# Attention scores of a transformer block: q and k kept fp32 on chip in 32-partition quadrants, in place of a three-way bf16 split stacked through DRAM

## What is computed

```python
q = split_heads(x @ Wq.T)            # (B, 16 heads, T, 16)
k = split_heads(x @ Wk.T)
v = split_heads(x @ Wv.T)
q = _apply_rope(q)                   # t * cos + rot(t) * sin
k = _apply_rope(k)
scores = jnp.einsum('bhtd,bhsd->bhts', q, k) * scale
scores = jnp.where(causal[None, None], -jnp.inf, scores)
attn = jax.nn.softmax(scores, axis=-1)
out = jnp.einsum('bhts,bhsd->bhtd', attn, v)
return out.transpose(0, 2, 1, 3).reshape(B, T, 256) @ Wo.T
```

## Time and profile before

| what | value |
|---|---|
| runs of the kernel | 3821.51 us median of 3 (3818.33 to 3827.86) |
| span of the profiled execution, first to last instruction | 3828.2 us |
| PE matmul busy | 3068.0 us, 80% |
| DVE busy | 2449.9 us, 64% |
| POOL busy | 1463.4 us, 38% |
| ACT busy | 1276.0 us, 33% |
| mean granted TensorE clock | 0.897 of 2.4 GHz |
| moved by DMA | 106.01 MB |

### The profile page before, as it was taken

One profiled execution on the slowest core, in us unless ns is written; L12 is line 12 of the kernel. 1 busy time (PEld: TensorE's weight loads), 2 busy tenths in 40 slices (PEclk: granted clock), 3 DMA queues, 4 the chain that ended last, 5 costly groups with the idle time before them and its releaser, 6 DMA issues. The chain is left out here.

```text
span 3828.2 us, 47386 instructions
## 1 busy us (share of the span) xinstructions
PE 3068.0 (80%) x17056; PEld 1877.3 (49%) x17056; DVE 2449.9 (64%) x5133; ACT 1276.0 (33%) x2632; POOL 1463.4 (38%) x1323
## 2 busy tenths in 40 slices
PE   2689767897688975899758997589885898858898
PEld 1235743456434564345633456335573355723557
DVE  5755767547585485854758547585575855768556
ACT  1353033530345312452125521255211542216422
POOL 2224442244513445134551345413454134541344
PEclk9799987999889987899978999789997999969999
DMA  4400023000330003200041000410005000050000
GB/s 129 78 2 1 1 59 64 2 1 1 67 56 2 1 1 78 45 2 1 1 93 30 1 1 1 96 28 2 0 1 109 15 2 0 7 115 2 1 1 12
DMA packets 46763, 106.01 MB, mean 28 GB/s; under 512 B 9713, under 2 KB 30225, under 8 KB 43281
## 3 DMA queue, kind: packets, MB, share of 16 engines
q1 hardware_dynamic: 46480, 102.24, 13.0%
HBM read 65.51 MB, written 35.91 MB: 26 GB/s over the span
## 5 line engine op out<-in xcount | busy, mean ns | idle before, releaser
L803 DVE TENSOR_REDUCE mxp<-PB 128x1 f32<-128x512 f32 (+3 forms) x1536 | 753.2, 549 | 274.7 <-PE PB L1053 182.2
L656 ACT ACTIVATE arena<-PB 128x512 f32<-128x512 f32 (+3 forms) x1536 | 650.5, 509 | 651.3 <-PE PB L1064 646.5
L1050 PE MATMUL PB<-arena 96*128 96x512 bf16 (+3 forms) x1536 | 542.7, 383 | 286.2 <-DMA arena<-parts 214.8
L535 POOL TENSOR_SCALAR_AFFINE_SELECT arena<-arena 128x512 f32<-128x512 f32 x256 | 162.7, 636 | 981.4 <-ACT arena L656 981.0
L1064 PE MATMUL PB<-arena 99*128 99x512 bf16 (+3 forms) x1536 | 467.6, 344 | 16.7 <-DMA arena<-augT 9.5
L1050 PEld LDWEIGHTS PB<-arena 96*128 96x128 bf16 x1536 | 160.8, 106 | 631.6 <-DVE mxp L803 349.2
L1079 PE MATMUL PB<-arena 128*32 128x512 f32 (+3 forms) x3072 | 343.4, 520 | 15.5 <-ACT attn L642 13.7
L1273 PE MATMUL PB<-arena 128*128 128x128 f32 x1792 | 243.4, 293 | 98.3 <-DVE arena L965 98.2
L520 POOL TENSOR_TENSOR hl<-arena,hh 128x512 fp32r<-128x512 f32 x192 | 248.6, 1295 | 192.5 <-ACT hh L673 192.5
L1135 PE MATMUL PB<-xh,wgu 128*128 128x512 f32 x768 | 306.9, 400 | 11.4 <-DVE xres L761 10.8
L1135 PE MATMUL PB<-xl,wgu 128*128 128x512 f32 x768 | 303.3, 395 | 0.0
(11 more groups left out here) (138 smaller groups left out, 5536.3 us busy)
## 6 DMA issues: line engine op xcount, KB each, us to landing
arena<-parts SPq DMA_DIRECT2D x112, 256.0 KB, 10.5
parts<-arena SPq DMA_DIRECT2D x96, 256.0 KB
arena<-parts SPq DMA_DIRECT2D x16, 768.0 KB, 16.0
xres<-in_x SPq DMA_DIRECT2D x16, 512.0 KB, 4.3
arena<-parts SPq DMA_DIRECT2D x16, 512.0 KB, 18.5
out<-xres SPq DMA_DIRECT2D x16, 512.0 KB, 2.9
wlow_dram<-wlow SPq DMA_DIRECT2D x1, 2304.0 KB, 6.8
arena<-augT SPq DMA_DIRECT2D x96, 8.0 KB, 1.8
```

Source lines behind the costliest of these rows:

```text
L656: act.activation(pt[:, U % 3, h, 0:n], bank("score", t)[:, 0:n], ACT.Exp, scale=DH ** -0.5).then_inc(act_emptied, 1)
L803: dve.reduce_max(mxp[:, g % 2, h, col:col + 1], bank("max", g * NPC + k)[:, 0:n], axis=AX.X).then_inc(dve_emptied, 1)
L1050: last = mm(ps[:, 0:n], qst[0:AUG, h, 128 * i:128 * i + 128], kst[0:AUG, h, s0:s0 + n], start=True, stop=not diag)
```

## The change

q and k are made in another layout: one product tile holds, for each of four heads, 16 partitions of q and then 16 of k, a quadrant of 32 partitions per head (the host interleaves the weights as `wqk`). DVE shuffles the tile by 8 channels (L719 of the changed kernel) and multiplies by cos into `qk` (L720); POOL multiplies by sin and adds (L466, L469). A second shuffle on DVE swaps the halves of each quadrant into `kq` (L727), which has k where `qk` has q. All of it is fp32. The bf16 split, the DRAM tensor, `qst`, `kst`, the memset of ones and ACT's part in this are gone; a DMA writes the row of ones in `kq`.

`max_items` (L981) and `score_items` (L1000) issue four heads after each other. Each is an fp32 product over 16 partitions (17 with the maximum's row) of another quadrant, so that the four heads lie in four row groups of the array. The four causal products follow the four heads. The negated maxima are one fp32 row: two small operations on DVE, a transpose in fp32 and four DMAs of 4 KB per group. In the plan of banks four max items stand together, then four score items.

```diff
+QK_ORDER = [(0, 0), (1, 0), (0, 1), (1, 1), (2, 0), (2, 1), (3, 0), (3, 1)]
+KEYS_READY = [3, 4, 6, 8]
+SWAP = [(i + 16) % 32 for i in range(32)]
-LAG = 12
-DELAY = NPC + LAG
+NQ = len(PIECES)
+LAG = 3
+DELAY = NQ + LAG
...
-    for t in range(NSC + DELAY):
-        if t < NSC:
-            p.append(("max", t, "dve"))
-        if NPC <= t < NSC + NPC and t % NPC == AUG_AT:
-            p.append(("aug", t // NPC - 1, "dve"))
+    for t in range(NG * NQ + DELAY):
+        if t < NG * NQ:
+            p.extend(("max", HG * t + h, "dve") for h in range(HG))
+        if NQ <= t < NG * NQ + NQ and t % NQ == 0:
+            p.append(("aug", t // NQ - 1, "dve"))
         if t >= DELAY:
-            p.append(("score", t - DELAY, "act"))
+            p.extend(("score", HG * (t - DELAY) + h, "act") for h in range(HG))
...
-        qst = take(8192, bf16, 0).rearrange("p (h t) -> p h t", h=NH)
-        kst = take(8192, bf16).rearrange("p (h t) -> p h t", h=NH)
+        qk = take(4096, f32, 0).rearrange("p (g t) -> p g t", g=NG)
+        kq = take(4096).rearrange("p (g t) -> p g t", g=NG)
...
+                    sp.wait_ge(keys_set, len(QK_ORDER))
+                    for h in range(HG):
+                        sp.dma_start(kq[32 * h + DH:32 * h + DH + 1, :, :],
+                                     consts[2].rearrange("a (g t) -> a g t", g=NG)).then_inc(ones_loaded, 16)
                     for g in range(NG):
                         wait_emptied(sp, "aug", g)
-                        for r in range(3):
-                            sp.dma_start(qst[AUG + r:AUG + r + 1, HG * g:HG * g + HG, :],
-                                         augT[32 * r:32 * r + 32, g % 2, :]).then_inc(aug_loaded[g], 16)
+                        for h in range(HG):
+                            sp.dma_start(qk[32 * h + DH:32 * h + DH + 1, g, :],
+                                         augT[NT * h:NT * h + NT, g % 2, :]).then_inc(aug_loaded[g], 16)
...
+                    for e, (g, f) in enumerate(QK_ORDER):
                         cols = slice(HALF * f, HALF * f + HALF)
+                        pool.wait_ge(rot_shuffled, e + 1)
+                        pool.tensor_tensor(turned[e % 2], turned[e % 2], rope[:, 1, cols], ALU.mult).then_inc(rot_sin, 1)
+                        pool.wait_ge(rot_sin, e + 1)
+                        wait_emptied(pool, "qk", e)
+                        pool.tensor_tensor(qk[:, g, cols], qk[:, g, cols], turned[e % 2], ALU.add).then_inc(roped, 1)
...
+                        dve.stream_shuffle(turned[e % 2], bank("qk", e)[:, :], ROTATE).then_inc(rot_shuffled, 1)
+                        dve.tensor_tensor(qk[:, g, cols], bank("qk", e)[:, :], rope[:, 0, cols],
+                                          ALU.mult).then_inc(dve_emptied, 1)
+
+                    def keys(e):
+                        g, f = QK_ORDER[e]
+                        cols = slice(HALF * f, HALF * f + HALF)
+                        dve.wait_ge(roped, e + 1)
+                        dve.stream_shuffle(kq[:, g, cols], qk[:, g, cols], SWAP).then_inc(keys_set, 1)
...
+                    def max_items(g, j):
+
+                        i, s0, n, col = PIECES[j]
+                        for h in range(HG):
+                            k = g * NPC + HG * j + h
+                            r = slice(32 * h, 32 * h + DH)
+                            diag = s0 + n == 128 * (i + 1)
+                            wait_bank(pe, "max", k)
+                            last = mm(bank("max", k)[:, 0:n], qk[r, g, 128 * i:128 * i + 128], kq[r, g, s0:s0 + n],
+                                      start=True, stop=not diag)
+                            if not diag:
+                                last.then_inc(filled, 1)
                         if diag:
+                            for h in range(HG):
+                                k = g * NPC + HG * j + h
+                                mm(bank("max", k)[:, n - 128:n], identb[:, :], causal[:, :],
+                                   start=False, stop=True).then_inc(filled, 1)
+
+                    def score_items(g, u):
+
                         j, f = UNITS[u]
                         t0 = max(HALF * f, 128 * j)
                         n = HALF * (f + 1) - t0
+                        for h in range(HG):
+                            k = g * NPC + HG * u + h
+                            r = slice(32 * h, 32 * h + DH + 1)
+                            wait_bank(pe, "score", k)
+                            mm(bank("score", k)[:, 0:n], kq[r, g, 128 * j:128 * j + 128], qk[r, g, t0:t0 + n],
+                               start=True, stop=True).then_inc(filled, 1)
```

More of the change, by code:

```diff
@@ L630, in _ @@
                     act.wait_ge(arena_set, 2)
-                    for e in range(4):
-                        high(e)
-                    mid(3)
                     for n in range(4):
                         v_out(n)
-                    for e in range(4, 8):
-                        high(e)
-                    mid(7)
                     def pv_out(g):
@@ L798, in _ @@
+                    def keys(e):
+                        g, f = QK_ORDER[e]
+                        cols = slice(HALF * f, HALF * f + HALF)
+                        dve.wait_ge(roped, e + 1)
+                        dve.stream_shuffle(kq[:, g, cols], qk[:, g, cols], SWAP).then_inc(keys_set, 1)
+                    for e in range(len(QK_ORDER)):
                         rotary(e)
+                        if e >= 2:
+                            keys(e - 2)
+                    keys(len(QK_ORDER) - 2)
@@ L1041, in v_item @@
                         last.then_inc(filled, 1)
-                    def max_item(g, k):
-                        h, (i, s0, n, col) = max_item_of(k)
-                        h += g * HG
-                        wait_bank(pe, "max", g * NPC + k)
-                        ps = bank("max", g * NPC + k)
-                        diag = s0 + n == 128 * (i + 1)
-                        last = mm(ps[:, 0:n], qst[0:AUG, h, 128 * i:128 * i + 128], kst[0:AUG, h, s0:s0 + n],
-                                  start=True, stop=not diag)
-                        if diag:
-                            last = mm(ps[:, n - 128:n], identb[:, :], causal[:, :], start=False, stop=True)
-                        last.then_inc(filled, 1)
-                    def score_item(g, k):
-                        u, h = k // HG, g * HG + k % HG
+                    def max_items(g, j):
[9 more added lines that the diff above has]
+                                last.then_inc(filled, 1)
+                        if diag:
+                            for h in range(HG):
[3 more added lines that the diff above has]
+                    def score_items(g, u):
                         j, f = UNITS[u]
@@ L1061, in score_item @@
                         n = HALF * (f + 1) - t0
-                        wait_bank(pe, "score", g * NPC + k)
-                        ps = bank("score", g * NPC + k)
-                        mm(ps[:, 0:n], kst[0:AUG + 3, h, 128 * j:128 * j + 128], qst[0:AUG + 3, h, t0:t0 + n],
-                           start=True, stop=True).then_inc(filled, 1)
+                        for h in range(HG):
+                            k = g * NPC + HG * u + h
[3 more added lines that the diff above has]
+                               start=True, stop=True).then_inc(filled, 1)
                     def pv(g, u):
@@ L1373 @@
         masks.append((p // (2 * m) == t // (2 * m)) & (p % (2 * m) < m))
+    arrays["one"] = np.ones((1, NG * T), np.float32)
     arrays["ci"] = np.concatenate(masks + [p == q], 1).astype(np.int32)
```

192 lines of the change are left out of this document (51 added, 141 removed).

## The result

| what | before | changed |
|---|---|---|
| time | 3824.69 us median of 4 runs (3818.33 to 3829.77) | 4643.74 us median of 4 runs (4641.87 to 4651.55) |
| ratio to before | | 1.2144, 95% interval 1.2126 to 1.2162 |
| span of the profiled execution | 3828.2 us | 4642.8 us |
| mean granted TensorE clock | 0.897 | 0.74 |

The change makes the kernel 21% slower. The forecast was 3950 us with a range from 3790 to 4250: the sign was right, the size was wrong by 694 us, and the time lies above the range.

A forecast was written before the change was run, and what follows sets the result against it. PE, or a chain through it, was taken to bound most stages. Per batch -20 (front) + 28 (mixed) + 5 (maxima) + 3 (scores) = +16 us, times eight +128, on 3821.5: 3950 us, range 3790 to 4250.

The forecast's parts named there:

- The front: From the q and k products to the first reduction: without split and DRAM trip, 20 us less per batch.
- The mixed stage: Where maxima, scores and `pv` mix: waits for banks make a step 3.65 us against 2.81, 28 us more per batch.
- rival 3: TensorE stays at 1.2 GHz in the mixed stage: +2.0 us a step, +65 per batch, 4470 us; chance 0.07.
- Maxima alone: Stage of row maxima only, before the first score: fills and reductions chain, +5 us per batch, bounds 0 and +12.
- Scores alone: Last stage of a batch: scores wait two by two for ACT, +3 us, bounds 0 and +5.
- Rival 1: Weight loads or passes of row groups queue on PE: 4130 us for loads, 4290 for passes; chance 0.15.
- rival 2: The row groups do not run side by side at all: mixed step 6.7 us, about 5000 us; chance 0.05.
- Rival 4: The bank wait does not bind, so a mixed step is PE's 2.57 us: 3600 us; chance 0.13.
- The tipping point: Length of a mixed-stage step under which the batch gains: 3.17 us.
- the forecast's sum of +16 us per batch: All attention stages of a batch: -20 + 28 + 5 + 3 = +16 us, times eight +128 us.

The follow-up runs named there:

- The bursts: The changed kernel with unused fp32 products of 512 columns ahead of the batch loop, in groups of 16 or 32 rows or all 128 rows, waiting for nothing: 4889.41 us.

## Why the prediction was wrong

- **The front, -20 us per batch** (bounds 18 to 21): -20.9. POOL's pair of operations, forecast 2.6 us, took 2.58, and the first reduction comes 37.8 us after the first statistics where "about 40" was said.
- **The mixed stage, 3.65 us a step** (3.25 to 4.1): 5.79, and this is the step that failed. Its chain was right: at the higher level it takes 3.77 us with the same waits, the last two score heads wait for the reductions of heads 0 and 1 as forecast, and halving these takes 0.42 us off. What failed is that each of its terms for PE came from rows at 2.4 GHz, on the premise that the stage would keep that clock. The stage ran at 1.2 GHz from end to end. That was **rival 3**, priced at 4470 us with a chance of 0.07. For this stage its price was near: it added +65 us per batch, and the clock's share measured here is +66.7. It left the last stage and the maxima out, and its reason, that TensorE would wait more, is only part of the cause.
- **Why rival 3 got 0.07.** The prediction judged the clock by waits: a stage with waits for ACT is granted 0.94, so this one would be too. Every product in those rows works on 96, 99 or 128 rows of the array. The change puts all row-group products on 16 or 17 rows of each 32, and no row of the trace before has such a one. The bursts show that this alone can keep the clock from rising, without any wait, and the kernel with 32 rows shows that undoing it alone brings the clock of the mixed stage back. Waits count beside it: the bursts of 16 rows behind full products hold 2.4 GHz, and the stage does not.
- **Maxima alone, +5 us** (0 to +12): +11.9, at the upper bound, which was set with the lower clock in mind. The causal products with their changes of shape carry it: without them it is 29.2 us even at 0.50. The rows do not: with 32 it is still +11.4.
- **Scores alone, +3 us** (0 to +5): +11.6, outside its bounds; with 32 rows +2.1. Again the clock.
- **Rival 1** (loads or passes queue) and **rival 2** (groups not side by side): refuted by eight loads in 0.52 us at the lower clock and 0.31 at the higher, and by 0.87 us for a round of four. **Rival 4** (the bank wait doesn't bind): refuted; at the full clock and with the banks in another order a step is 3.45 us still. The tipping point, 3.17 us, was passed by the kernel with bf16 maxima and full products alone, in its one batch at full clock: 102.5 / 33 = 3.11 us.
- With the clock out of the way in the mixed and the last stage, the forecast's sum of +16 us per batch stands against +24.6 in the kernel with 32 rows (-20.6 + 11.4 + 31.7 + 2.1), and 3950 us against 4031.

Where did the expected gain go? The 20.9 us of the front came back in full. At the higher clock the chain of the mixed stage takes 31.7 us away (21.3 with the other order of banks and no causal products), and the causal products cost 11.9 in the maxima-only stage; the lower clock then adds 66.7 us in the mixed stage and about 9.5 in the last.

**What stays open.** By what rule rows and waits together set the clock; the changes of shape were not varied apart from them. Whether the rows' contents matter (in the kernel with 32 rows the 15 rows added to the scores hold zeros in `kq` and k in `qk`, and yet the clock rose; rows of zeros on both sides weren't tried). What makes the clock drop for a few microseconds in the kernels with bf16 maxima was not found; the kernel before has such drops too (at 662.2 and 696.4 in the second batch). A seventh circulating bank wasn't tried, since `pv` holds the other two.

## What to carry to other kernels

When a change makes the products of a long stage narrower in rows of the array, price the stage at both clock levels, and look in the trace for products as narrow before trusting the clock of today. If a tile has unused rows, let the product run over them with zeros or constants on one side: a round of 512 columns took 0.87 us with 16 rows in each group and with 32, and here the extra rows were worth 613 us. And when groups of four share a ring of six banks, write down which item lies six places back for each: the two that fall on banks just filled put the reader's latency into every step.

## What the runs showed of the hardware

- Four row groups of 16 rows, fp32, without a gap for 34.5 us, did not lift TensorE from 1.2 to 2.4 GHz; four groups of 32 rows behind them were at 2.4 GHz after 4.6 us; one group of 32 rows lost it after 5.5 us. The same groups of 16 rows behind full products kept it for 17.45 us.
- In the kernel, 32 rows in four groups ran at 0.97 in the mixed stage and at 0.50 in the maxima-only stage, and there at 0.55 to 0.88 when DVE's reductions were half as wide.
- Four groups of 16 rows cost the time of one full product: a round of 512 columns fp32 takes 0.87 us at 2.4 GHz, as one product of 128 rows does, and 34.5 / 20 = 1.73 us at 1.2 GHz.
- Loads of row groups overlap: eight end 0.31 us after the first has begun at 2.4 GHz (696.93 in the kernel with 32 rows), 0.52 us at 1.2 GHz.
